# A four-layer graph network on one core: order of the first layer and its borders, and another form of the first layer's softmax weights

## The chip, the cores and the metric

One core of one Trainium2 chip. The metric is the device time of one execution in microseconds; the median over several executions is compared. The core has five engines with queues of their own: TensorE (PE, matmuls and transposes), VectorE (DVE), ScalarE (ACT), GpSimd (POOL, here the queue that issues indirect transfers) and SyncE (SP, here the queue that issues plain transfers).

## The reference

50,000 nodes with 128 features pass through four graph layers over 12,500 edges, sorted by target node. Each layer's result is added to its input and normalized over the features.

```python
x = _layernorm(x + L0(x, edges, edge_weight, edge_attr))   # attention with a softmax over the edges of a target
x = _layernorm(x + L1(x, src, dst))                        # mean of neighbours, two linear maps, relu
x = _layernorm(x + L2(x, src, dst, edge_type_8))           # one of 8 matrices for each edge, summed by target
x = _layernorm(x + L3(x, src, dst, edge_type_3, node_type_3))
...
# L0, for the 4 heads of an edge:
alpha = (q_s[dst] + k_s[src] + e_s) * inv_sqrt_c + gate * edge_weight
alpha = jnp.where(alpha >= 0, alpha, 0.2 * alpha)
ex = jnp.exp(alpha - amax[dst])
denom = segment_sum(ex, dst)
out = segment_sum(v[src] * ex / (denom[dst] + 1e-16), dst) + bias
```

## The kernel before

**Two streams of work.** The dense stream takes all nodes in 100 blocks of 500 rows (125 partitions x 4 x 128 features) through all four layers, for nodes without edges and as a base for the rest. Step d of it (numbered in the code as `d`) works on three blocks at once: block d enters layer one, block d - 3 (LAG) layer two and three, block d - 6 the last layer. The edge stream takes the 12,500 edges in 25 chunks of 500, layer by layer: 25 chunks of the first layer, then 25 of the second, and so on. The two streams are interleaved by hand: two dense steps go with each first-layer chunk, one with each chunk of the second and third layer, none with the fourth. Every engine has its own written-out program; semaphores tie them together. Nothing is planned by a scheduler: the order of calls in each engine's block is the order of work.

**First layer, one chunk c.** GpSimd gathers source and target rows (`sources0`, `targets0`, four indirect transfers each) and issues five more for the table of slots. TensorE transposes the rows (`turn_sources0`, `turn_targets0`, L1380) into one PSUM bank `pt`, ScalarE takes them out (`evacuate_sources` to `st`, `evacuate_targets` to `dt`, L1145), and TensorE adds three products into `pc`: `score_features`, `score_sources` (L1494) and `score_targets` (L1500). ScalarE writes 0.2 of the scores (`slopes0`, L1151), VectorE takes the larger (L842). The softmax is computed as a running one along the edges: L844 scans the running maximum (in the profile every scan has its helper's line, L831), which a mask of -1e30 resets where a new target begins; L845 subtracts the score from the maximum of the edges before. ScalarE splits the difference d in two by Relu (`differences0`, L1156 and L1157) and takes two exponents (`weights0`, L1162 and L1163): the old sum is scaled by one of them (`wb`) and the new term by the other (`wa`). Two more scans (`weight_sums`, `value_sums`) carry the sums on. TensorE turns them back (`back0`, L1514, L1518), ScalarE takes out the denominators (`sums0`), VectorE divides and adds (`target_rows0`, L867 to L871).

**The dense step.** VectorE's `read(d)` adds the bias (L791), takes the result of layer two out of PSUM bank group `po` (L796), selects the node type's result (L799, L800) and forms the last sum (L802); `measure` and L764, L767 make the variances. ScalarE's `first_roots` turns these into seeds of 1/sqrt, VectorE's `scales` (L778 to L781) finishes them, ScalarE normalizes rows (L1074). TensorE's `dense_turns` transposes (`turn_rt`, `turn_xt`), ScalarE evacuates (`evacuate_rt`, `evacuate_xt`), and `dense_products` writes `po`: `biased_slots` (L1386) and the type products (L1391) need `read(d + 2)` to be through and `rt`; `z_products` (L1451) need `xt`. `read(d + 3)` waits for them.

**What sets the order around the change.** In the first layer's loop each engine runs this for chunk c:

```python
# TensorE, the end of a chunk           # ScalarE, the ends of a chunk
turn_xt(2 * c + 1)                      first_roots(s, 8)
turn_targets0(c + 2)                    slopes0(c + 1)
score_targets(c + 2)                    ...
dense_products(2 * c + 1)               evacuate_xt(2 * c + 1)
                                        evacuate_targets(c + 2, 0, 0, dt, ACT.Copy)
```

VectorE's loop is: `source_rows0(c)` (L880), `read(2c)`, statistics, `target_rows0(c - 1)`, `read(2c + 1)`, statistics, `weight_sums(c)` (scan), `scales` (L778 on), `value_sums(c)` (scan), `scores(c + 1)` (L841 to L845).

**Borders.** After the last first-layer chunk ScalarE writes all rows and results before `only_dense(2 * EC)` takes `rt` out; the second layer's gathers wait for the last target rows in memory (`landed(1)`). Before the third layer TensorE runs `dense_products(d - 2)` ahead of `turns2(0)`. GpSimd gathers the node types of the targets (`types2`, array `ntd_all`, 100 transfers): 8 after the second layer's gathers, 3 in each of the third layer's 25 chunks, and the last 17 between the third layer's gathers and `landed(3)`, ahead of the fourth layer's. They are needed first at L1046, when the fourth layer begins. ScalarE runs the last `dense_chain` before it takes out `st` of the fourth layer's chunk 1.

## Time and profile before

| | |
|---|---|
| median of three executions | 1655.96 us (1653.0 to 1656.04) |
| the profiled execution | 1652.15 us, span 1650.4 us |
| mean granted TensorE clock | 0.929 of full |
| busy share of the span | PE 84%, DVE 86%, ACT 67%, POOL 75% |
| chain that ended last | PE 44%, DVE 32%, ACT 12%, issue 10% |

How to read it: a busy share is a mean over stages with different limits. PE is TensorE's matmul, PEld its weight load. In a timeline row the columns are the start in us, the duration in us, the engine, the line, the operation with output and inputs, how many were merged, and in brackets the idle time ahead of it with what ended it. `issue` as a releaser means that the profile shows nothing that was waited for. Instructions on one engine overlap a little, so the next may start before the last has ended. L12 is line 12 of the kernel before.

### The profile page before, as it was taken

What the parts mean: (1) busy time and instruction counts of PE and PEld (TensorE: products, weight loads), DVE (VectorE), ACT (ScalarE), POOL (GpSimd) and SP (SyncE); (2) the same over time, 40 slices, a digit from 0 to 9 for tenths busy, and PEclk for the clock granted to TensorE, in tenths of its full rate; (3) what the DMA queues carried; (4) which work ended last, traced back from release to release, by engine and by line L of the source; (5) the groups of instructions that cost most, each with busy time, mean ns of one, the idle gap of its engine ahead of it and who ended that gap; (6) DMA issues with size and microseconds to landing.
All of it is one profiled execution on the core that took longest, in us unless ns stands there. A gap on an engine that the chain in (4) does not pass through costs nothing.

```text
span 1650.4 us, 22899 instructions
## 1 busy us (share of the span) xinstructions
PE 1388.8 (84%) x6078; PEld 890.6 (54%) x6078; DVE 1419.0 (86%) x3056; ACT 1110.9 (67%) x2769; POOL 1230.3 (75%) x910
## 2 busy tenths in 40 slices
PE   3788877788778868777776899999996899999995
PEld 2455554555545546666665555555553455555552
DVE  5899899999899879999998799999995677777773
ACT  1678788887788787888888577777774344444441
POOL 7888888877777857888874567777778488888873
PEclk9798888988889879999998999999998899999997
DMA  7344444434444256767675455556554344344320
GB/s 172 94 100 102 111 109 110 112 91 115 111 113 105 58 139 177 189 179 192 182 187 149 131 149 164 156 157 165 151 133 111 83 97 96 96 97 97 96 70 20
DMA packets 165797, 205.06 MB, mean 124 GB/s; under 512 B 66825, under 2 KB 97920, under 8 KB 165668
## 3 DMA queue, kind: packets, MB, share of 16 engines
q1 hardware_dynamic: 108068, 179.45, 40.0%
q0 software_dynamic: 57600, 24.15, 9.0%
q8 instruction: 50, 0.82, 0.2%
q14 instruction: 79, 0.65, 0.2%
HBM read 147.12 MB, written 70.80 MB: 132 GB/s over the span
## 4 chain that ended last, share of the span: by engine, by line
PE 44%; DVE 32%; ACT 12%; issue 10%; POOL 1%; DMA 1%; SPq 0%; DVEq 0%; POOLq 0%; ACTq 0%
PE po L1391 23%; DVE bst L756 8%; DVE masked L969 6%; PE pt L1380 5%; PE pc L1500 3%; PE po L1386 3%; ACT x L1074 3%; DVE run L831 2%; PE po L1451 2%; DVE y L796 2%; DVE po L799 2%; DVE sel L802 2%; DVE po L800 2%; ACT do L1074 2%; PE pa L1672 1%
## 5 line engine op out<-in xcount | busy, mean ns | idle before, releaser
L536 POOL DMA_INDIRECT xs<-target_rows,slot_all x236 | 322.2, 1365 | 140.9 <-issue 60.9
L1074 ACT ACTIVATE x<-y,nmr,rst 125x128 f32<-125x128 f32 x800 | 322.5, 483 | 29.6 <-issue 18.4
L1391 PE MATMUL po<-wnt,rt 128*125 128x384 f32 x800 | 297.4, 518 | 0.0
L1380 PE MATMUL pt<-ident,x 125*128 125x125 f32 x800 | 122.3, 276 | 110.5 <-issue 110.5
L1391 PEld LDWEIGHTS po<-wnt,rt 128*125 128x125 f32 x800 | 162.7, 206 | 96.9 <-issue 21.2
L1391 PE MATMUL po<-wnt,run 128*125 128x384 f32 x600 | 201.5, 486 | 0.0
L543 POOL DMA_INDIRECT out_rows<-do,last_all x100 | 146.5, 1465 | 63.0 <-issue 40.6
L1380 PEld LDWEIGHTS pt<-ident,x 125*128 125x128 f32 x800 | 93.1, 145 | 148.4 <-issue 147.1
L536 POOL DMA_INDIRECT xs<-in_x,src_all x100 | 143.2, 1432 | 34.7 <-issue 33.8
L1074 ACT ACTIVATE do<-yd,nmr,rst 125x128 f32<-125x128 f32 x400 | 163.5, 483 | 5.4 <-DVE nmr L781 4.6
L1074 ACT ACTIVATE res<-sel,nmr,rst 125x128 f32<-125x128 f32 x400 | 163.7, 484 | 2.6 <-DVE nmr L781 1.8
L1627 PE MATMUL pb<-masked,wr 128*128 128x500 f32 x350 | 156.5, 588 | 2.2 <-DVE masked L969 2.2
L536 POOL DMA_INDIRECT slot_all<-slot_d,src_all x100 | 131.9, 1319 | 30.5 <-issue 30.5
L536 POOL DMA_INDIRECT ntd_all<-in_ntype,dst_all x100 | 129.4, 1294 | 30.5 <-issue 30.5
L543 POOL DMA_INDIRECT slot_d<-eid,last_all x100 | 128.5, 1285 | 30.5 <-issue 30.2
L756 DVE BATCH_NORM_STATS2 bst<-y 125x6 f32<-125x256 f32 x400 | 143.1, 420 | 3.8
L1391 PEld LDWEIGHTS po<-wnt,run 128*125 128x125 f32 x600 | 108.9, 188 | 68.7 <-issue 0.6
L1140 ACT ACTIVATE st<-pt 128x500 f32<-128x500 f32 x50 | 29.3, 585 | 142.1 <-issue 95.1
L536 POOL DMA_INDIRECT xdb<-target_rows,slot_all x64 | 86.6, 1352 | 44.2 <-issue 29.3
L536 POOL DMA_INDIRECT xd<-in_x,dst_all x68 | 94.9, 1396 | 27.2 <-issue 19.2
L1386 PE MATMUL po<-ball,ones_bf 128*125 128x384 bf16 x412 | 102.2, 379 | 13.0 <-DVE sel L802 13.0
L1451 PEld LDWEIGHTS po<-wab,xt 128*125 128x125 f32 x800 | 101.5, 188 | 19.8
(190 smaller groups left out, 3035.1 us busy)
## 6 DMA issues: line engine op xcount, KB each, us to landing
xin<-in_x SPq DMA_DIRECT2D x100, 224.0 KB
out_rows<-res SPq DMA_DIRECT2D x100, 224.0 KB
source_rows<-so SPq DMA_DIRECT2D x75, 224.0 KB
target_rows<-do SPq DMA_DIRECT2D x75, 224.0 KB
xs<-source_rows SPq DMA_DIRECT2D x59, 224.0 KB
same<-same_d SPq DMA_DIRECT2D x50, 250.0 KB
rel<-in_etype SPq DMA_DIRECT2D x50, 250.0 KB
xd<-target_rows SPq DMA_DIRECT2D x46, 224.0 KB
```

Of the source, the lines that this page charges most:

```text
L536: return nc.gpsimd.indirect_dma_start(out=to, out_offset=None, in_=table, in_offset=bass.IndirectOffsetOnAxis(ap=index, axis=0), bounds_ch ...
L543: return nc.gpsimd.indirect_dma_start(out=table, out_offset=bass.IndirectOffsetOnAxis(ap=index, axis=0), in_=of, in_offset=None, bounds_ch ...
L756: last = V.bn_stats(to, y[:, j:j + 2, :].rearrange("p j d -> p d j"))
L796: last = V.scalar_tensor_tensor(out=y1[(d - LAG) % 4][:, :, :], in0=of_z, scalar=0.0, in1=x1[(d - LAG) % 4][:, :, :], op0=ALU.max, op1=ALU ...
L969: V.scalar_tensor_tensor(out=masked[:, r, :], in0=rel[b][:, :], scalar=float(r), in1=st[:, :], op0=ALU.is_equal, op1=ALU.mult).then_inc(q[ ...
L1074: last = A(to[:, j, :], y[:, j, :], ACT.Identity, scale=rst[s][:, k:k + 1], bias=nmr[s][:, k:k + 1])
L1380: last = nc.tensor.transpose(tile_of(to, j), rows_[:, j, :], ident[0:R, 0:R])
L1386: mm(po[0:R, j * 512:j * 512 + NT * D], ones_bf[:, 0:R], ball[:, :, :].rearrange("k s d -> k (s d)"), start=True, stop=False, skip_group_c ...
L1391: last = mm(po[0:R, j * 512:j * 512 + NT * D], left(j), wnt[:, k, :, :].rearrange("k t d -> k (t d)"), start=start, stop=stop, skip_group_ ...
L1451: last = mm(po[0:R, j * 512 + NT * D:(j + 1) * 512], xt[:, j, :], wab[:, 0, :], start=False, stop=True, skip_group_check=True)
L1500: mm(pc[:, 0:C], qs[:, :], dt[:, :], start=False, stop=True).then_inc(q["pA"], 1)
L1627: mm(pb[:, 0:C], wr[:, r, :], masked[:, r, :] if r else st[:, :], start=r == 0, stop=r == REL - 1).then_inc(q["pM"], 1)
```

## The change

- VectorE's form of the weights (`scores`): the mask is used at the edge itself, not one edge ahead. The scan is now max(run + mask, score). Then three operations: `wb` = run before + mask, completed before the next; `wa` = score - run; `wb` = `wb` - run. ScalarE takes the exponent of each; the two Relus and their semaphore `eR` are gone, and with them one of the two transfers of the mask array, and a memset.
- ScalarE's loop in the first layer: `evacuate_targets(c + 1)` comes after `first_roots` of chunk c, in place of the end of the chunk before.
- TensorE's loop in the first layer: the second dense product of a chunk is split; biased slots and type products come before `turn_targets0(c + 2)`, the z products between it and `score_targets(c + 2)`.
- End of the first layer on ScalarE: `evacuate_rt`, `evacuate_xt` and `first_roots` of the next dense step come between the rows and before the results.
- Second to third layer on TensorE: `turns2(0)` before `dense_products(d - 2)`.
- GpSimd: 15 of the type gathers are issued in the second layer's chunks 20 to 24, so that 2 are left of the 17 ahead of `landed(3)`.
- Third to fourth layer on ScalarE: `evacuate_sources(1, 3, 0)` before the last `dense_chain`.

```diff
@@ -66,7 +66,7 @@
...
     d_rows = [nc.dram_tensor(f"target_rows{i}", [E, D], F32).ap() for i in (1, 2, 3)]
     same_d = nc.dram_tensor("same_d", [1, E], F32).ap()
-    start_d = nc.dram_tensor("start_d", [1, E + 1], F32).ap()
+    start_d = nc.dram_tensor("start_d", [1, E], F32).ap()
     rdeg_d = nc.dram_tensor("rdeg_d", [1, E], F32).ap()
@@ -172,7 +172,7 @@
...
         SOONER = 10
 
-        SINGLE = ("tS tD eS eD eL pA pB pR vA vE vL eX eR nS nD nF yb eN sc", "tS tD eS eD pR vA nS nD rd vF",
+        SINGLE = ("tS tD eS eD eL pA pB pR vA vE vL eX nS nD nF yb eN sc", "tS tD eS eD pR vA nS nD rd vF",
                   "tS eS pM pR vA vM nD nF nS", "tS tD eS eD pM pR vM vA eX vN nD rd bs xb")
@@ -240,8 +240,7 @@
...
             sp.wait_ge(s_prep, 1)
             row = lambda a: a.rearrange("o (p t) -> (o p) t", t=PM)
-            sp.dma_start(row(start_d[0:1, 0:E]), start_p[:, :]).then_inc(s_scr, 16)
-            sp.dma_start(start_d[0:1, E:E + 1], start_p[0:1, 0:1]).then_inc(s_scr, 16)
+            sp.dma_start(row(start_d), start_p[:, :]).then_inc(s_scr, 16)
             sp.dma_start(w1t[:, :, :], W1T).then_inc(s_w2, 16)
@@ -255,7 +254,7 @@
...
                 sp.dma_start(ea[b][0:ED, :], eattrT[:, cols(c)]).then_inc(q["aux"][b], 16)
                 sp.dma_start(ea[b][ED:ED + 1, :], eweight[0:1, cols(c)]).then_inc(q["aux"][b], 16)
-                sp.dma_start(aux[b][:, :], start_d[0:1, bass.ds(c * C + 1, C)].broadcast_to([D, C])).then_inc(q["aux"][b], 16)
+                sp.dma_start(aux[b][:, :], to_all(start_d, c)).then_inc(q["aux"][b], 16)
 
@@ -269,7 +268,7 @@
...
                     sp.dma_start(rows(d_rows[0])[c][part, :], flat(do[b])[part, :]).then_inc(q["stD"][b], 16)
 
-            sp.wait_ge(s_scr, 32)
+            sp.wait_ge(s_scr, 16)
             features0(0)
@@ -633,6 +632,9 @@
...
                         pool.wait_ge(s_slot[k], 16 * T * (n - 1))
                     slots1(i, i + 1, s_slot[k])
+                if SOONER * T + 3 * c >= EC * T:
+                    types2(typed, typed + 3)
+                    typed += 3
             types2(typed, typed + 2 * T)
@@ -694,7 +696,6 @@
...
             V.memset(carry[:, :], 0.0)
             step(V.memset(run[:, :, :], 0.0))
-            V.memset(run[:, 0, 0:1], -BIG)
             V.tensor_scalar(start_p[:, :], same_p[:, :], -1.0, BIG, ALU.add, ALU.mult).then_inc(s_prep, 1)
@@ -841,8 +842,10 @@
...
                 V.tensor_tensor(score, score, pc[:, 0:C], ALU.max).then_inc(q["vL"], 1)
                 dve.wait_ge(q["vL"], c + 1)
-                step(scan(run, 0, score, aux[b][:, :], ALU.max, ALU.add))
-                V.tensor_tensor(wb, run[:, 0, 0:C], score, ALU.subtract).then_inc(q["vE"], 1)
+                step(scan(run, 0, aux[b][:, :], score, ALU.add, ALU.max))
+                step(V.tensor_tensor(wb, run[:, 0, 0:C], aux[b][:, :], ALU.add))
+                V.tensor_tensor(wa, score, run[:, 0, 1:C + 1], ALU.subtract)
+                V.tensor_tensor(wb, wb, run[:, 0, 1:C + 1], ALU.subtract).then_inc(q["vE"], 1)
 
@@ -1123,8 +1126,12 @@
...
             def dense_chain(d):
 
+                first_roots(chain_of(d) % 2, 4)
+                chain_rows(d)
+
+            def chain_rows(d):
+
                 k = chain_of(d)
-                first_roots(k % 2, 4)
                 act.wait_ge(s_ln, k + 1)
@@ -1150,17 +1157,11 @@
...
                 A(score, pc[:, 0:C], ACT.Copy, scale=0.2).then_inc(q["eL"], 1)
 
-            def differences0(c):
+            def weights0(c):
                 q = ph[0]
                 act.wait_ge(q["vE"], c + 1)
-                A(wa, wb, ACT.Relu)
-                A(wb, wb, ACT.Relu, scale=-1.0).then_inc(q["eR"], 1)
-
-            def weights0(c):
-                q = ph[0]
-                act.wait_ge(q["eR"], c + 1)
-                A(wb, wb, ACT.Exp, scale=-1.0)
-                A(wa, wa, ACT.Exp, scale=-1.0).then_inc(q["eX"], 1)
+                A(wb, wb, ACT.Exp)
+                A(wa, wa, ACT.Exp).then_inc(q["eX"], 1)
 
@@ -1183,13 +1184,14 @@
...
             evacuate_targets(0, 0, 0, dt, ACT.Copy)
             slopes0(0)
-            differences0(0)
             weights0(0)
...
                 s = chain_of(2 * c) % 2
                 first_roots(s, 8)
+                if c >= 1 and there(c + 1):
+                    evacuate_targets(c + 1, 0, 0, dt, ACT.Copy)
                 if there(c + 1):
@@ -1199,7 +1201,6 @@
...
                 if there(c + 1):
                     evacuate_rt(2 * c)
-                    differences0(c + 1)
                     evacuate_xt(2 * c)
@@ -1217,12 +1218,13 @@
...
                     act.wait_ge(s_tail, 1)
                     target_rows0(c, TAIL, 0)
+                    evacuate_rt(2 * EC - 2)
                     source_rows0(c, s)
+                    evacuate_xt(2 * EC - 2)
+                    first_roots(chain_of(2 * EC) % 2, 4)
                     results_of(2 * c, s, 2)
                     results_of(2 * c + 1, s, 3)
-                if there(c + 2):
-                    evacuate_targets(c + 2, 0, 0, dt, ACT.Copy)
-            only_dense(2 * EC)
+            chain_rows(2 * EC)
             evacuate_dense(2 * EC - 1)
@@ -1350,8 +1352,8 @@
...
             messages3(0)
             targets3(0)
+            evacuate_sources(1, 3, 0)
             dense_chain(NC + 2 * LAG - 1)
-            evacuate_sources(1, 3, 0)
             act.wait_ge(s_x1, NC)
@@ -1553,10 +1555,16 @@
...
                         score_sources(c + 2)
                     turn_xt(2 * c + 1)
+                    if 2 * c + 1 >= LAG:
+                        type_products(2 * c + 1)
+                    else:
+                        pe.wait_ge(s_read, 2 * c + 4)
+                        biased_slots()
                     if there(c + 2):
                         turn_targets0(c + 2)
+                    z_products(2 * c + 1).then_inc(s_z, 1)
+                    if there(c + 2):
                         score_targets(c + 2)
-                    dense_products(2 * c + 1)
 
@@ -1628,9 +1636,9 @@
...
             d = block_of(1, EC)
             dense_turns(d - 2)
-            dense_products(d - 2)
             pe.wait_ge(ph[1]["rd"], EC)
             turns2(0)
+            dense_products(d - 2)
             relations2(0, range(REL // 2))
...
```

## Rows read from the trace of the kernel before

**Rows 1.** Busy time in stretches: us, then PE, PEld, DVE, ACT, POOL; clock, DMA, GB/s.
```profile
80.00:560.00 480.00, 393.27 (x1760) 253.70 (x1758) 437.55 (x898) 385.78 (x976) 385.39 (x281) 0.87 0.44 105
...
615.00:885.00 270.00, 212.96 (x1423) 173.36 (x1423) 261.16 (x657) 234.15 (x598) 211.22 (x159) 1.00 0.68 180
...
935.00:1245.00 310.00, 302.86 (x1225) 181.33 (x1224) 301.12 (x656) 225.35 (x578) 223.13 (x167) 1.00 0.58 152
...
1295.00:1640.00 345.00, 334.81 (x1110) 190.15 (x1108) 262.49 (x464) 134.69 (x289) 256.98 (x183) 0.99 0.35 85
```

**Rows 2.** Waits, 60 to 560 us: total us, times, longest.
```profile
DVE tmp L778 <- issue: 14.1, 13, 4.0
...
DVE y L796 <- PE po L1451: 11.2, 19, 1.2
...
DVE tmp L778 <- ACT seed L1083: 7.2, 7, 1.1
```

**Rows 3.** Timeline of VectorE, first layer.
```profile
311.15 1.26 DVE L831 TENSOR_TENSOR_SCAN run<-masked,run,aux 128x500 f32<-128x500 f32 x1
...
313.04 0.68 DVE L880 TENSOR_TENSOR so<-xs,bias_bc 125x512 f32<-125x512 f32 x1
...
324.74 0.69 DVE L802 SCALAR_TENSOR_TENSOR sel<-x,po 125x512 f32<-125x512 f32 x1
...
330.02 0.19 DVE L778 SCALAR_TENSOR_TENSOR tmp<-seed 125x32 f32<-125x32 f32 x1 [1.01 <-ACT seed L1083]
...
332.80 0.67 DVE L842 TENSOR_TENSOR masked<-masked,pc 128x500 f32<-128x500 f32 x1
...
563.50 0.67 DVE L842 TENSOR_TENSOR masked<-masked,pc 128x500 f32<-128x500 f32 x1
```

**Rows 4.** Timeline of ScalarE, first layer.
```profile
329.02 0.59 ACT L1145 ACTIVATE dt<-pt 128x500 f32<-128x500 f32 x1 [1.25 <-PE pt L1380]
```

**Rows 5.** Timeline of TensorE, first layer.
```profile
318.26 0.81 PE L1386 MATMUL po<-ball,ones_bf 128*125 128x384 bf16 x4
...
321.50 1.04 PE L1451 MATMUL po<-wab,xt 128*125 128x128 f32 x8
322.80 1.01 PE L1494 MATMUL pc<-st,ks 128*128 128x500 f32 x2
...
329.66 2.03 PE L1500 MATMUL pc<-dt,qs 128*128 128x500 f32 x2 [0.68 <-ACT dt L1145]
331.49 1.48 PE L1386 MATMUL po<-ball,ones_bf 128*125 128x384 bf16 x4
...
335.96 1.04 PE L1451 MATMUL po<-wab,xt 128*125 128x128 f32 x8
```

**Rows 6.** Stretch view of TensorE alone: us, PE busy, granted clock, DMA, GB/s.
```profile
328.00:330.00 2.00, 1.32 (x5) 0.50 0.87 267
```

**Rows 7.** Timeline of GpSimd, first layer.
```profile
311.87 1.62 POOL L536 DMA_INDIRECT xs<-in_x,src_all  x1 [0.30 <-issue]
```

**Rows 8.** Timeline of TensorE, first border.
```profile
599.40 1.06 PE L1380 MATMUL pt<-ident,x 125*128 125x125 f32 x4 [11.45 <-issue]
```

**Rows 9.** Group of the type gathers; then timelines of GpSimd and TensorE, second border.
```profile
L536 POOL DMA_INDIRECT ntd_all<-in_ntype,dst_all x100 | 129.4, 1294 | 30.5 <-issue 30.5
...
900.88 1.27 POOL L536 DMA_INDIRECT xs<-target_rows,slot_all  x1 [17.16 <-DMA target_rows<-do]
...
910.83 1.46 PE L1386 MATMUL po<-ball,ones_bf 128*125 128x384 bf16 x4
...
916.62 0.59 PE L1380 MATMUL pc<-ident,xs 125*128 125x125 f32 x4
```

**Rows 10.** Timelines of GpSimd and TensorE, third border.
```profile
1262.04 1.27 POOL L536 DMA_INDIRECT xdb<-target_rows,slot_all  x1 [0.30 <-issue]
...
1269.68 1.07 PE L1380 MATMUL pt<-ident,xdb 125*128 125x125 f32 x4 [4.09 <-issue]
...
1285.89 2.03 PE L1672 MATMUL pa<-st,wet 128*128 128x500 f32 x2 [7.40 <-ACT st L1140]
```

## The prediction

> **What bounds the kernel now.** I read the stages first: the view by stretches [rows 1] splits the span into four layers with short borders between them. In the first layer (80 to 560 us) VectorE is busy 437.6 of 480 us, TensorE 393.3, ScalarE 385.8 and GpSimd 385.4, with TensorE granted 0.87 of full clock; in the second and third VectorE has 261.2 of 270 and 301.1 of 310 us; in the fourth TensorE has 334.8 of 345. So VectorE is nearest to the limit in three layers and TensorE in the last. Time saved on another engine counts only where one of these waits for it.
>
> Next I read the first layer's waits [rows 2]: in 500 us VectorE waits 14.1 + 7.2 us for the seeds of L778 and 11.2 us for the z products at L796. Its timeline [rows 3] gives the period: L842 starts at 332.80 and at 563.50, ten chunks apart, 23.07 us each. The waits are 32.5 us over 21.7 such periods, 1.50 a chunk, so VectorE's own work is about 21.57 us. Short delays hidden by overlapping instructions are not in that sum; between 21.4 and 21.6 is my bracket, 21.45 my value.
>
> Then ScalarE and TensorE [rows 4 to 6]: ScalarE stands 1.25 us before the evacuation dt at 329.02, in front of the seeds, so the seeds come late. TensorE runs the type products only after score_targets, and part of this at the lower of its two clocks: the same two 500-column matmuls take 1.01 us at 322.80 and 2.03 us at 329.66 (1.2 GHz, granted clock 0.50, where before it was 2.4). At the borders I read TensorE's and GpSimd's timelines [rows 8 to 10].
>
> **First layer, VectorE's arithmetic.** The scan (1.26 us at 311.15) keeps its length. Before, one subtraction follows it and then L880, which does not wait for that subtraction: from the scan's end, 312.41, to L880 at 313.04 are 0.63 us, 0.60 for the subtraction and 0.03 for the hand-over. Now an addition that must complete comes first, then two subtractions. The addition costs a whole operation of this size, 0.68 us, and a hand-over, 0.72 with rounding; each subtraction 0.60 [rows 3]. Added: 0.72 + 0.60 = 1.32 us a chunk. ScalarE loses two Relus of the size of dt (0.59 us in [rows 4]); that is worth nothing by itself, since ScalarE already waits. VectorE's floor is then 21.45 + 1.32 = 22.77 us.
>
> **First layer, the order.** Moving the dt evacuation behind first_roots puts the seeds in front of ScalarE's wait, and they hide under the weight scan. Moving the type products ahead of turn_targets0 removes the z wait, which also lets back0 start earlier. So the 1.50 us of waits go. What is late next is the chain that now hangs from the second read: the read's last instruction (324.74, ends 325.43) releases type_products(2c+1); then come the target transposes, dt on ScalarE, score_targets, the slopes, and L842. From there to L842 are 332.80 - 325.43 = 7.37 us, of which 1.01 is the wait for the seeds at 330.02 [rows 3]; room 6.4 us. The chain at the high clock [rows 4, 5]: 3.24 us (biased slots and types, 318.26 to 321.50) + 0.55 (four transposes, half the 1.07 of the slow ones in [rows 10]) + 0.59 (dt) + 1.01 (scores) + 0.59 (slopes, same shape as dt) + about 0.2 for hand-overs = 6.2 us, with z beside dt. It just fits. At the lower clock in part it does not: the same products took 4.47 us (331.49 to 335.96), 1.23 more, and the scores 1.02 more. So the stall is 0 to 2.2 us a chunk. The clock fell before after TensorE had stood for most of the time from 323.8 (the end of the row at 322.80) to 329.66 [rows 5, 6]; in the new order it pauses before the same products, for the rt evacuation and the read, but more briefly. I take 0.45 us, nearer to the clean row, because the score matmuls should mostly run at the high clock again. Period 22.77 + 0.45 = 23.22 against 23.07: +0.15 x 22 chunks = +3 us. Bounds: -7 us (no stall) and +42 us (2.2 in every chunk).
>
> The three chunks of the ramp I cost at nothing, within 2 us either way. The single start-mask transfer instead of two, the memset gone and the shifted mask are before the first chunk, beside the weight loads; nothing, and at most 1 us either way.
>
> **A lock on GpSimd.** GpSimd issues 13 indirect transfers a chunk, 385.4 us / 281 = 1.37 us each [rows 1] and 0.31 between two [rows 9]: 21.8 us of the 23.07. The one that starts at 311.87, inside the scan, took 1.62 us [rows 7] against 1.29 on the mean for the type gathers [rows 9], so a scan holds it up by about 0.33 us. The Trainium skill, "SBUF — State Buffer", section "Who interferes with whom", says that a VectorE instruction with two SBUF inputs blocks a GpSimd instruction that reads SBUF, and for its full length. The trace agrees in that row. By the row, one more delay of 0.33 us fits in GpSimd's slack and the sum stays. By the rule, all 1.3 us of new two-input work could be added to GpSimd, 21.8 + 1.3 = 23.1 us a chunk, and the first layer could not win anything: +1 us in place of -7 us for the case without stalls.
>
> **First border.** TensorE stood 11.45 us before the transpose at 599.40 [rows 8], because the rt evacuation came after all rows and results. It now comes some 4 us earlier, and the dense products with it. But the second layer's first transposes need GpSimd's gathers, which wait for the last target rows, and those are not moved. ScalarE's own work also stays in the way. Only the 1 us by which results no longer delay its next rows is left: -0.9 us; bounds 0 and -4.
>
> **Second border.** turns2(0) moves ahead of the dense products that ran from 910.83 to 916.62: 5.8 us earlier at most [rows 9]. Against it: 15 type gathers move into the end of the second layer, where GpSimd had only 8; each costs 1.29 + 0.31 = 1.60 us. Twelve of the 15 and the 8 follow the last row gather. The 8 before ended 17.16 us ahead of 900.88, when the first gather started, at 883.72; twelve more and a last row gather that starts some 0.7 us later make 883.72 + 12 x 1.60 + 0.7 = 903.6, so the first gather comes 2.8 us later. A group of four gathers needs 7.64 us from its start to TensorE (1262.04 to 1269.68, [rows 10]), so turns2(0) can run at 911.3, 5.3 us sooner. Then the displaced dense products push the relation products and with them st of the next chunk, which takes back some 1.6 us: -3.7 us; bounds 0 and -5.8. The layer behind is full on VectorE, so this gain stays.
>
> **Third border [rows 10].** Of the 17 type gathers between the layers 15 are gone, 24 us of GpSimd. The first row gather (1262.04) can go as soon as the last rows have landed. TensorE stood 4.09 us before its transpose at 1269.68 and was busy before, so 4.1 us is the most that this brings; I take all of it. Second, st of chunk 1 is taken out before the last dense chain: TensorE's 7.40 us before 1285.89 shrink to an evacuation and hand-over, 0.8 us: -6.6 us. Behind these pauses the matmuls ran at 1.2 GHz (2.03 us for two); some of them now run at 2.4 GHz: -0.8 us. Together -11.5 us; bounds -4 (only one of the two) and -16. The fourth layer is bound by TensorE [rows 1], so its start shifts the end one for one.
>
> **Sum.** +3 - 0.9 - 3.7 - 11.5 = -13.1 us. The profiled execution took 1652.15 us (span 1650.4), so 1639.1 by it. It is 3.8 us below the median of 1655.96, and two of the three runs shown lie at 1656; the forecast goes by the median: 1655.96 - 13.1 = 1642.9, rounded to 1642 because the sum has more room below.
>
> **Rivals.**
> (1) No stall: the first layer reaches VectorE's floor, -7 us, total -23: 1633. For it: the chain fits by 0.2 us at the high clock. Against it: that margin, and GpSimd's lock. Chance 0.20.
> (2) The lock makes GpSimd the bound, first layer +1 us, total -15: 1641; told from the forecast only by whether the transfers are long. Chance 0.06.
> (3) The borders' gains are hidden anyway: the second and third layers' queues (row stores, loads, ScalarE's order) hold them to -4 us in the third border and nothing else; with +3 us: 1655, or 1651 if half of the second border stays. For it: each border moves one thing out of several. Against it: TensorE's waits of 7.40 and 4.09 us name just what is moved. Chance 0.13.
> (4) The other side, slower: in the first layer the chain from the read over type products, dt, scores and slopes runs at the lower clock in every chunk. At 1.6 us of stall: (22.77 + 1.6 - 23.07) x 22 = +28.6, total +12.5: 1668. It decides from 1.05 us a chunk, where 22 x (22.77 + 1.05 - 23.07) = 16.5 eats the borders' 16.1. For it: the products follow TensorE's pauses. Against it: these are shorter than before. Chance 0.11.
> The forecast has 0.50.
>
> **How the numbers follow.** 0.2%, about 3.3 us, is what can be told from no change. Faster: 0.50 + 0.20 + 0.06 and 0.07 of case 3, 0.83; same: 0.06 of case 3; slower: 0.11. The likeliest case's own range is 1634 to 1650 (stall 0.1 to 0.8 us, third border -8 to -15). The range of 8 in 10 takes in most of cases 1 and 3: 1629 to 1655.
>
> **What would show it.** VectorE: L778 without a wait in the first layer, 1.32 us more between the scan and L880's start. L842 waiting on ScalarE's slopes: my stall; over 1.05 us a chunk, case 4. Period near 22.8: case 1. GpSimd without any wait for VectorE and a period equal to VectorE's: case 2. Borders: TensorE's pauses before the last first-layer transpose, before the first relation product's source and before the fourth layer's second message product shorter by some 4, 5 and 6.6 us; GpSimd's first third-layer gather 2.8 us later relative to the layer's end. The forecast is wrong if the first layer moves by more than 15 us or the third border brings less than 8.

## The result, and the profile after

The changed kernel takes 1660.03 us (median of 7 runs, 1658.3 to 1662.74) against 1654.32 us of the kernel before in as many runs beside it (1653.0 to 1656.04). The ratio is 1.0041 with a 95% interval of 1.0031 to 1.0050: slower by 5.7 us, where 13.1 us less and 1642 were forecast. The profiled execution took 1658.97 us, span 1657.2.

The starts of the scans (VectorE, one per chunk and layer, listed by line for each kernel) mark the stages in both traces. Each stretch runs from the start of one scan to that of another:

| stretch | before, us | after, us | difference | forecast |
|---|---|---|---|---|
| first layer, first to last scan | 533.2 | 554.7 | +21.5 | +3 |
| first border | 48.6 | 47.5 | -1.1 | -0.9 |
| second layer | 274.5 | 276.5 | +2.0 | 0 |
| second border | 46.0 | 46.2 | +0.2 | -3.7 |
| third layer | 312.9 | 313.1 | +0.2 | 0 |
| third border and fourth layer | 365.3 | 350.1 | -15.2 | -11.5 |

The start (-0.8) and the tail (0) make it +6.8 us of span. The first and the third border did what was forecast or more, the second gained nothing, and the first layer took it all back.

The view by stretches of the changed kernel (columns as in [rows 1]; the later three lie where the layers lie now):

```profile
80.00:560.00 480.00, 372.73 (x1696) 241.36 (x1693) 443.13 (x900) 351.02 (x894) 372.43 (x269) 0.86 0.44 103
636.00:905.00 269.00, 212.55 (x1431) 173.76 (x1431) 259.32 (x652) 231.34 (x590) 212.21 (x161) 1.00 0.70 180
957.00:1265.00 308.00, 300.71 (x1216) 180.26 (x1214) 299.30 (x650) 225.17 (x577) 217.97 (x162) 1.00 0.57 151
1302.00:1647.00 345.00, 334.19 (x1108) 189.81 (x1106) 266.40 (x468) 135.24 (x291) 260.13 (x185) 0.99 0.36 88
```

In the first row no engine is full: VectorE stands for 37 of 480 us, although it has 1.3 us more to do in each chunk. In the waits of the changed kernel (60 to 560 us, columns as in [rows 2]) VectorE's seeds are gone, and among the long entries are waits of ScalarE for TensorE and of TensorE for ScalarE:

```profile
ACT xt L1120 <- PE pt L1382: 54.6, 23, 3.0
...
ACT dt L1152 <- PE pt L1382: 39.3, 21, 3.7
PE pa L1508 <- ACT den L1171: 36.4, 21, 1.9
...
ACT masked L1158 <- PE pc L1502: 25.1, 21, 1.2
```

One period of it, ScalarE first (the timelines of the changed kernel; L1158 slopes, L1077 rows and results, L1171 denominators, L1163 and L1164 the exponents):

```profile
320.68 0.59 ACT L1158 ACTIVATE masked<-pc 128x500 f32<-128x500 f32 x1 [1.20 <-PE pc L1502]
...
324.24 1.64 ACT L1077 ACTIVATE res<-sel,nmr,rst 125x128 f32<-125x128 f32 x4
...
325.84 0.16 ACT L1171 ACTIVATE den<-pa 125x4 f32<-125x4 f32 x1
...
329.01 0.59 ACT L1120 ACTIVATE xt<-pt 128x500 f32<-128x500 f32 x1 [2.55 <-PE pt L1382]
...
331.17 0.59 ACT L1147 ACTIVATE st<-pt 128x500 f32<-128x500 f32 x1 [0.55 <-PE pt L1382]
...
337.81 0.56 ACT L1114 ACTIVATE rt<-pt 128x500 f32<-128x500 f32 x1
...
342.79 0.59 ACT L1152 ACTIVATE dt<-pt 128x500 f32<-128x500 f32 x1 [1.81 <-PE pt L1382]
344.57 0.59 ACT L1158 ACTIVATE masked<-pc 128x500 f32<-128x500 f32 x1 [1.20 <-PE pc L1502]
```

and TensorE (L1382 turns, L1508 values, L1491 the features' scores, L1388 and L1393 biases and types, L1453 z, L1502 the targets' scores):

```profile
323.48 0.79 PE L1382 MATMUL pt<-ident,x 125*128 125x125 f32 x4
326.14 2.01 PE L1508 MATMUL pa<-st,wv 128*128 128x500 f32 x2 [1.87 <-ACT den L1171]
327.94 1.04 PE L1382 MATMUL pt<-ident,x 125*128 125x125 f32 x4
328.77 1.88 PE L1491 MATMUL pc<-ea,es 65*128 65x500 f32 x2
...
338.47 0.62 PE L1382 MATMUL pt<-ident,x 125*128 125x125 f32 x4 [1.97 <-issue]
338.93 0.82 PE L1388 MATMUL po<-ball,ones_bf 128*125 128x384 bf16 x4
339.58 2.74 PE L1393 MATMUL po<-wnt,rt 128*125 128x384 f32 x8
342.16 0.59 PE L1382 MATMUL pt<-ident,xdb 125*128 125x125 f32 x4
342.59 1.04 PE L1453 MATMUL po<-wab,xt 128*125 128x128 f32 x8
343.46 1.07 PE L1502 MATMUL pc<-dt,qs 128*128 128x500 f32 x2
```

Read as one chain these rows close on themselves: slopes, rows, results and denominators on ScalarE (320.68 to 326.0); values and the turn of x1 on TensorE (326.14 to 328.98); xt, the exponents, st (after 0.55 us of wait for TensorE), rows, the edge rows and rt on ScalarE (329.01 to 338.37); turn, types and the targets' turn on TensorE (338.47 to 342.75); dt; the scores; and the next slopes at 344.57, 23.89 us on. No link of it is on VectorE, whose own work is 22.73 us (the period less its waits of 0.87 at L842 and 0.29 at L797). It waits at the end of the chain:

```profile
345.19 0.15 DVE L842 COPY run<-run 128x1 f32<-128x1 f32 x1 [0.87 <-ACT masked L1158]
```

TensorE's granted clock in it (columns as in [rows 6]). TensorE had stood 1.54 us ahead of the turning back at 322.18; the clock falls shortly before 324, at the end of the short work that follows and before the pause for the denominators begins. The values, a turn and the features' scores run at the lower clock, the types' products no longer do.

```profile
322.18 0.67 PE L1516 MATMUL pb<-ident,run 128*125 128x128 f32 x4 [1.54 <-DVE masked L843]
```

```profile
322.00:324.00 2.00, 1.82 (x16) 0.95 0.15 33
324.00:326.00 2.00, 0.27 (x2) 0.50 0.15 32
...
328.00:330.00 2.00, 2.00 (x7) 0.50 0.52 75
330.00:332.00 2.00, 2.00 (x11) 0.84 0.96 216
```

At the third border of the changed kernel the two pauses of [rows 10] are gone or small, and the products run at 2.4 GHz:

```profile
1286.88 0.62 PE L1382 MATMUL pt<-ident,xdb 125*128 125x125 f32 x4
...
1293.97 1.10 PE L1680 MATMUL pa<-st,wet 128*128 128x500 f32 x2 [0.68 <-ACT st L1147]
```

At the second, GpSimd works through the moved types until the first gather, and TensorE gets its rows 11.64 us after that gather's start, at the lower clock (the rows that answer to [rows 9]):

```profile
924.06 1.27 POOL L535 DMA_INDIRECT ntd_all<-in_ntype,dst_all  x1 [0.30 <-issue]
925.64 1.27 POOL L535 DMA_INDIRECT xs<-target_rows,slot_all  x1 [0.30 <-issue]
```
```profile
937.28 1.07 PE L1382 MATMUL pc<-ident,xs 125*128 125x125 f32 x4 [3.78 <-issue]
```

### The profile page after: what moved, and what is told of

Its sections match the earlier page's. It is cut to its first block, busy times and chain, and to the rows that moved or that the text cites. A ratio compares the mean times of both kernels' runs of the same rounds, so it can differ in the third digit from the quotient of the medians.

```text
span 1657.2 us, 22897 instructions
## 1 busy us (share of the span) xinstructions
PE 1381.7 (83%) x6078; PEld 890.1 (54%) x6078; DVE 1450.1 (88%) x3105; ACT 1087.2 (66%) x2719; POOL 1235.3 (75%) x910
## 4 chain that ended last, share of the span: by engine, by line
PE 45%; DVE 35%; ACT 9%; issue 9%; DMA 1%; POOL 0%; SPq 0%; DVEq 0%; POOLq 0%; ACTq 0%
PE po L1393 23%; DVE bst L757 9%; DVE masked L972 6%; PE pt L1382 5%; ACT x L1077 4%; DVE run L832 3%; PE pa L1508 3%; PE po L1453 3%; ACT res L1077 2%; DVE po L801 2%; DVE sel L803 2%; PE pc L1491 2%; PE po L1388 2%; DVE y L797 2%; DVE po L800 2%
## 5 line engine op out<-in xcount | busy, mean ns | idle before, releaser
L1077 ACT ACTIVATE x<-y,nmr,rst 125x128 f32<-125x128 f32 x800 | 322.4, 482 | 28.9 <-DVE nmr L782 28.9
L1393 PE MATMUL po<-wnt,rt 128*125 128x384 f32 x800 | 283.2, 499 | 0.0
L1382 PE MATMUL pt<-ident,x 125*128 125x125 f32 x800 | 137.1, 300 | 101.7 <-issue 101.7
L1393 PE MATMUL po<-wnt,run 128*125 128x384 f32 x600 | 201.5, 487 | 0.0
L1393 PEld LDWEIGHTS po<-wnt,rt 128*125 128x125 f32 x800 | 153.6, 195 | 88.2 <-issue 7.8
L1382 PEld LDWEIGHTS pt<-ident,x 125*128 125x128 f32 x800 | 102.9, 156 | 152.4 <-issue 151.6
L535 POOL DMA_INDIRECT xs<-in_x,src_all x100 | 148.8, 1488 | 34.9 <-issue 33.9
L1077 ACT ACTIVATE do<-yd,nmr,rst 125x128 f32<-125x128 f32 x400 | 163.4, 482 | 5.4 <-DVE nmr L782 5.4
L1077 ACT ACTIVATE res<-sel,nmr,rst 125x128 f32<-125x128 f32 x400 | 163.7, 483 | 2.6 <-DVE nmr L782 2.6
L1393 PEld LDWEIGHTS po<-wnt,run 128*125 128x125 f32 x600 | 109.1, 188 | 68.6 <-issue 0.6
L535 POOL DMA_INDIRECT xd<-in_x,dst_all x68 | 93.3, 1372 | 37.5 <-DVE yd L874 19.3
L832 DVE TENSOR_TENSOR_SCAN run<-aux,run,masked 128x500 f32<-128x500 f32 x100 | 120.4, 1246 | 0.9
L1120 ACT ACTIVATE xt<-pt 128x500 f32<-128x500 f32 x100 | 58.3, 583 | 76.0 <-PE pt L1382 76.0
```

Source lines behind the costliest of these rows:

```text
L535: return nc.gpsimd.indirect_dma_start(out=to, out_offset=None, in_=table, in_offset=bass.IndirectOffsetOnAxis(ap=index, axis=0), bounds_ch ...
L832: return V.tensor_tensor_scan(m[:, k, 1:C + 1], data0, data1, m[:, k, 0:1] if start is None else start, op0, op1)
L1077: last = A(to[:, j, :], y[:, j, :], ACT.Identity, scale=rst[s][:, k:k + 1], bias=nmr[s][:, k:k + 1])
L1120: A(xt[:, :, :], by_tile(pt), ACT.Copy, bias=1.0).then_inc(s_xt, 1)
L1382: last = nc.tensor.transpose(tile_of(to, j), rows_[:, j, :], ident[0:R, 0:R])
L1393: last = mm(po[0:R, j * 512:j * 512 + NT * D], left(j), wnt[:, k, :, :].rearrange("k t d -> k (t d)"), start=start, stop=stop, skip_group_ ...
```

## The experiments

Two theories at the start. A: the new order in the first layer lengthens the loop through ScalarE and TensorE. B: the three VectorE operations do. Medians below are of each kernel's runs (4 to 11); the kernel before stood between 1652.7 and 1653.2 us beside them.

**The parts one by one.** Three kernels each take some hunks of the change on top of the kernel before, with all that belongs to them; of each a few lines.

Borders alone, the hunks at the three borders:

```diff
             targets3(0)
+            evacuate_sources(1, 3, 0)
             dense_chain(NC + 2 * LAG - 1)
-            evacuate_sources(1, 3, 0)
```

> The kernel before with all the changes at the borders (ScalarE's order at the end of the first layer, the type gathers of the second layer, the turns of the third layer's first chunk, the early evacuation in the fourth) and the first layer's loop and weights left as they were. Theory A (the first layer's loop lost what the borders gave): the first layer keeps its 533 us from the first to the last scan, the fourth layer with its border gives the 15 us that the changed kernel shows, the first border 1, the second nothing: 1638 to 1641 us, a ratio of 0.991. Rival B (the fourth layer's gain was an echo of the first layer's later end, since loads and gathers had more time): the border's gain is under 8 us here, and the kernel stays above 1646.

Measured 1638.3, ratio 0.9907 (0.9892 to 0.9922). From the last scan of the third layer to the last of the fourth are 350.4 us, as in the changed kernel: the gain there is the borders' own.

Weights alone, the hunks in `scores`, `weights0` and the start marks:

```diff
-                V.tensor_tensor(wb, run[:, 0, 0:C], score, ALU.subtract).then_inc(q["vE"], 1)
+                step(V.tensor_tensor(wb, run[:, 0, 0:C], aux[b][:, :], ALU.add))
+                V.tensor_tensor(wa, score, run[:, 0, 1:C + 1], ALU.subtract)
+                V.tensor_tensor(wb, wb, run[:, 0, 1:C + 1], ALU.subtract).then_inc(q["vE"], 1)
```

> The kernel before with the new form of the first layer's weights alone (three VectorE operations for one, two exponents for two cuts and two exponents, the marks not shifted by one), old order everywhere. Theory A (the new order of dt, types and targets turned TensorE's clock down in another place and lengthened the loop; the arithmetic costs what VectorE had free): 0 to +8 us, a period of 23.1 to 23.4 us, and ScalarE's two cuts gone shorten its chain. Rival B (the arithmetic alone costs the 21 us: 1.32 us of VectorE for each of 24 chunks, less what its waits gave, behind the scan and ahead of the exponents): +18 to +25 us, a period of 23.8 to 24.1.

Measured 1653.47, ratio 0.9999 (0.9990 to 1.0008): nothing, and B is refuted. The stretch from 80 to 560 us shows VectorE at 459.7 busy us (437.6 in [rows 1]):

```profile
80.00:560.00 480.00, 395.24 (x1758) 254.86 (x1756) 459.68 (x937) 365.77 (x932) 374.44 (x278) 0.87 0.46 104
```

Periods are 22.5 to 23.6 us (22.35 to 23.5 before). In one chunk of four VectorE now waits for nothing, and that period, 22.52 us, is its own work; in the others its waits are 0.33 to 0.68 us, where they were 1.0 to 1.8.

Order alone, the loop's hunks on ScalarE (dt behind the roots) and TensorE (types, targets' turn, z, scores), both shown by halves further below:

> The kernel before with the first layer's new order alone (ScalarE takes dt out after the roots of the next chunk, TensorE puts the targets' turn between the types' products and z, and the targets' scores after z), old weights, old borders. Theory A (the order is what lengthens the loop): +10 to +20 us, TensorE at the low clock from the values' products on and not in the types' products, and ScalarE waiting over 2 us for the turn of x1 ahead of xt. Rival B (the arithmetic alone costs it): within 3 us of the kernel before. Rival C (only both together lengthen it, as VectorE's slack is gone and the chain of dt, scores and slopes is long): within 5 us here and within 8 us with the weights alone.

Measured 1673.05, ratio 1.0119 (1.0103 to 1.0134): +19.8 us. The three parts are -14.9, +0.3 and +19.8, in sum +5.2; together they measured +5.7. Most periods here are 23.88 to 23.90 us, those of the changed kernel, though VectorE has 1.3 us less to do: it just waits more (1.60 us at L796 and 0.86 at L841). ScalarE's two cuts, which this kernel still has, fit into its wait for xt, 1.53 us instead of 2.55. So neither VectorE's nor ScalarE's own work sets the period.

The changed kernel with the denominators taken out sooner:

```diff
                 rows_of(2 * c, s, (4, 0))
+                sums0(c)
                 if there(c + 1):
                     results_of(2 * c, s, 2)
-                sums0(c)
```

> The changed kernel with one move: ScalarE takes the denominators out before it writes the results of the dense block, not after (1.64 us earlier). Theory A (the pause that TensorE makes for the denominators ahead of the values' products is what lets its clock fall, and the products and turns at the low clock make ScalarE wait for xt 2.55 us in every chunk): the pause of 1.87 us is down to 0.3 or less, the wait for xt under 1.5 us, the period 23.89 down to between 22.8 and 23.2, the whole 15 to 24 us under the changed kernel: 1636 to 1645. Rival B (the loop is bound by VectorE's arithmetic and by the chain dt, scores, slopes): the period stays at 23.7 or above, 1655 to 1660.

Measured 1651.35, ratio 0.9994 (0.9983 to 1.0004), some 8 us under the changed kernel by the ratios, where I expected 15 to 24. The wait for xt is down to 1.20 and 0.75 us in the two chunks of the middle, and the periods are no longer one value but 22.7 to 24.4 us. So the link is on the chain. But my reason was wrong: the pause for the denominators is 0.5 us or none (1.87 before this edit), and still the values run at the lower clock for most of their length in 14 of 17 chunks (1.6 to 2.01 us for two; 1.08 in the other three). That pause is not what lets the clock fall.

**The clock, and the halves of the order.** In the changed kernel TensorE now repeats a turn to fill its pause; the argument says how often, and the signal goes with the last:

```diff
-                    turn_rt(2 * c)
+                    turn_rt(2 * c, 5)
                     values0(c + 1)
```

> The changed kernel with its first turn of x3 in each chunk issued five times in a row instead of once (the same values into the same tile, signalled after the last), so that TensorE works through most of the 1.87 us in which it otherwise waits for the denominators. Nothing comes earlier by it on any engine. Theory A (what the pause costs is TensorE's clock: the values' products, a turn and the features' scores at 1.2 GHz take 2.4 us more than at 2.4 GHz and hand ScalarE xt 2.55 us late): the granted clock stays at 1.00 between the turn and the sources' turn, the period goes from 23.89 to between 22.8 and 23.3, the whole to 1636 to 1648. Rival B (the clock is an effect and not a cause, what counts is when the denominators come out): the period stays at 23.8 or above and the whole at 1657 to 1662.

Measured 1664.26, ratio 1.0067 (1.0052 to 1.0081), slower still, and outside both expectations. Two neighbouring chunks of its trace differ. In one the types' products run at 1.2 GHz and VectorE waits 1.77 us; in the next at 2.4 GHz and it waits 0.33:

```profile
196.31 1.49 PE L1388 MATMUL po<-ball,ones_bf 128*125 128x384 bf16 x4
197.58 3.80 PE L1393 MATMUL po<-wnt,rt 128*125 128x384 f32 x8
...
206.44 4.00 PE L1382 MATMUL pt<-ident,x 125*128 125x125 f32 x20
...
221.06 0.81 PE L1388 MATMUL po<-ball,ones_bf 128*125 128x384 bf16 x4
221.71 2.74 PE L1393 MATMUL po<-wnt,rt 128*125 128x384 f32 x8
```
```profile
204.25 0.15 DVE L842 COPY run<-run 128x1 f32<-128x1 f32 x1 [1.77 <-ACT masked L1158]
...
227.32 0.15 DVE L842 COPY run<-run 128x1 f32<-128x1 f32 x1 [0.33 <-ACT masked L1158]
```

The chunks take 24.69 and 23.07 us in turn for most of the layer. The difference is in the products ahead of the targets' turn, which take 1.7 us longer at the lower clock; where it falls is worth 1.6 us a chunk.

The edit also did harm of its own. The clock fell just after the start of the repeated turns (at 206.5), behind a pause of 1.54 us that ended at 205.13. At the lower clock the twenty turns take 3.5 to 4.4 us, in 19 of the 20 chunks from 86 to 547 us (2.33 in the other one), and so last longer than the pause that they were to fill: the denominators are out at 208.95, the values start at 210.27, and ScalarE waits 1.52 us for the last turn before it can take rt out. So this run shows what the clock is worth in the types' products. It doesn't show what the chain would be if the clock had stayed up, and neither theory is settled by its time.

ScalarE's half of the order, on the kernel before:

```diff
                 first_roots(s, 8)
+                if c >= 1 and there(c + 1):
+                    evacuate_targets(c + 1, 0, 0, dt, ACT.Copy)
...
-                if there(c + 2):
-                    evacuate_targets(c + 2, 0, 0, dt, ACT.Copy)
```

> The kernel before with ScalarE's half of the new order alone: dt is taken out after the roots of the next chunk and not before them; TensorE's order, weights and borders as before. Theory A (TensorE's half of the order lengthens the loop): no loss here; VectorE's wait for the roots (0.7 to 1.1 us in the chunks of before) is gone, dt is 0.5 us later: -12 to +2 us. Rival B (ScalarE's half lengthens it: scores and slopes come later by the roots' 0.5 us and everything behind them on ScalarE): +12 to +20 us, a period near 23.9.

Measured 1652.28, ratio 0.9998 (0.9989 to 1.0007): no loss. VectorE's wait for the seeds has become one for the slopes (0.77 us at L841), the periods are those of the kernel before.

TensorE's half, on the kernel before:

```diff
                     turn_xt(2 * c + 1)
+                    if 2 * c + 1 >= LAG:
+                        type_products(2 * c + 1)
...
                     if there(c + 2):
                         turn_targets0(c + 2)
+                    z_products(2 * c + 1).then_inc(s_z, 1)
+                    if there(c + 2):
                         score_targets(c + 2)
-                    dense_products(2 * c + 1)
```

> The kernel before with TensorE's half of the new order alone: the targets' turn stands between the types' products and z, the targets' scores after z; ScalarE's order as before, so that the roots now stand behind a dt that comes later. Theory A (this half lengthens the loop, since dt, scores and slopes follow 3 us of types' products): +15 to +25 us, and VectorE waits over 1.5 us for the roots in every chunk. Rival B (the half on ScalarE is what costs): within 4 us of the kernel before.

Measured 1680.19, ratio 1.0161 (1.0148 to 1.0175): +27.5 us, a little over the range. This half is the loss. The periods are 23.89 again, with VectorE waiting 2.17 us for the seeds behind a late dt. ScalarE's half takes some 8 us of it back in the order as a whole.

The changed kernel with the whole order undone (these two hunks taken back):

> The changed kernel with only the first layer's order undone (new weights, all borders as changed). Theory A (the order is the whole loss, and the parts add up): 0.9999 times 0.9907 of before, 1638 us give or take 2, 21 under the changed kernel. Rival B (weights and borders share a slack that each alone still finds): 1643 or more.

Measured 1638.21, ratio 0.9909 (0.9894 to 0.9925). The parts add up, and the order costs 21.8 us in the changed kernel.

**Which products.** TensorE's half puts types ahead of the targets' turn, and z ahead of the targets' scores. One kernel takes the first back:

```diff
                     turn_xt(2 * c + 1)
+                    if there(c + 2):
+                        turn_targets0(c + 2)
                     if 2 * c + 1 >= LAG:
                         type_products(2 * c + 1)
...
-                    if there(c + 2):
-                        turn_targets0(c + 2)
                     z_products(2 * c + 1).then_inc(s_z, 1)
```

> The changed kernel with the targets' turn back ahead of the types' products of the odd dense block; z still stands ahead of the targets' scores, ScalarE's order and all else as changed. Theory A (dt, and the scores and slopes behind it, are late because the turn follows 3.4 us of types' products): dt is 3 us earlier, but the scores still follow types and z; of the 21 us at most half comes back, 1648 to 1660, if what counts is when the scores come, and all of it, 1637 to 1643, if what counts is when the turn comes (it holds the tile from which ScalarE takes dt out ahead of everything of the next chunk). I take the first.

Measured 1725.7, ratio 1.0448 (1.0431 to 1.0466), 67 us slower than the changed kernel by the ratios, where I had expected a gain. It undoes half of a move and is worse than the whole: the targets' turn now waits for xt (1.44 us), which the types had covered, the types come behind it at the lower clock (3.74 us for eight, 2.74 in the changed kernel), and the scores still follow all of it. ScalarE, and VectorE behind it, wait for the scores:

```profile
ACT masked L1158 <- PE pc L1502: 101.4, 19, 6.0
DVE run L842 <- ACT masked L1158: 64.8, 18, 5.0
```

The other takes the second back:

```diff
+                    if there(c + 2):
+                        score_targets(c + 2)
                     z_products(2 * c + 1).then_inc(s_z, 1)
-                    if there(c + 2):
-                        score_targets(c + 2)
```

> The changed kernel with the targets' scores ahead of z in the odd dense block, so that only the types' products still stand ahead of the targets' turn. Theory A (it is these 3.4 us, at the head of the chain of targets' turn, dt, scores and slopes, that lengthen the loop; z runs while ScalarE takes dt out): ScalarE's wait for the slopes' scores is 1.2 to 1.9 us as before, the whole within 6 us of the changed kernel's 1660. Rival B (z ahead of the scores is the costly half): the first layer gets back 15 us or more, 1645 or less.

Measured 1659.37, ratio 1.0033 (1.0021 to 1.0045), within 2 us of the changed kernel; the slopes' wait is 1.20 us as expected. In sum z ahead of the scores costs nothing, though the loop is another one: periods of 25.3, 23.4 and 23.0 us in turn, and the values at the higher clock in about half of the chunks. By both kernels what counts is that the types stand between the turn of x1 and the scores. A kernel with z alone there was not tried.

**Shortening the chain instead.** If the chain from rt to the slopes binds, the remedy is on ScalarE: on the kernel with changed borders, old weights and TensorE's old order,

```diff
                     source_rows0(c, s)
+                    evacuate_rt(2 * c + 1)
                     if c >= 1:
                         target_rows0(c - 1, s, 7)
-                    evacuate_rt(2 * c + 1)
-                    results_of(2 * c + 1, s, 3)
                     evacuate_xt(2 * c + 1)
+                    results_of(2 * c + 1, s, 3)
```

> The kernel before with the changed borders and another change of order in the first layer, on ScalarE alone: in the odd dense block rt is taken out ahead of the edge targets' rows and xt ahead of the results (old weights, TensorE's order as before). The turn of x1 should come 1.6 us earlier and the targets' turn 1.6 us or more. Theory A (the loop follows the chain xt, targets' turn, dt, scores, slopes, and the clock falls in TensorE's pause ahead of it): VectorE's waits of 1.5 us go down to 0.7 or less, the period from 23.07 to between 21.8 and 22.6, the whole to 1612 to 1630. Rival B (the period follows the dense blocks' chain of z, read, roots and rows, which this doesn't shorten): 1636 to 1640, as the borders alone.

Measured 1607.78, ratio 0.9724 (0.9711 to 0.9738), better than the range. The turn of x1 waits 0.53 us (2.06 in the kernel before), and in two of three chunks VectorE waits for nothing: a period of 21.2 to 21.4 us, its own work, and 22.3 in the third. Which of the two moves, rt or xt, carries it was not tried.

```profile
331.08 0.57 ACT L1114 ACTIVATE rt<-pt 128x500 f32<-128x500 f32 x1
331.55 1.65 ACT L1077 ACTIVATE do<-yd,nmr,rst 125x128 f32<-125x128 f32 x4
333.09 0.58 ACT L1120 ACTIVATE xt<-pt 128x500 f32<-128x500 f32 x1
```
```profile
331.76 0.62 PE L1390 MATMUL pt<-ident,x 125*128 125x125 f32 x4 [0.53 <-issue]
```

The same with the weights' hunks on top:

> The kernel with changed borders and rt and xt taken out earlier (1607.8 us, a period of 21.3 in which VectorE waits for nothing), now with the new form of the weights too. Theory A (the arithmetic cost nothing in the old loop only because that was bound by the hand-overs between ScalarE and TensorE; here VectorE is the bound): VectorE's 1.28 us more for each of 24 chunks are paid in full, a period of 22.6 to 22.8, 1635 to 1641. Rival B (the three operations overlap with each other and with waits, and ScalarE's two cuts less give it back): within 6 us of 1607.8.

Measured 1628.82, ratio 0.9846 (0.9832 to 0.9859): 20 to 21 us more than without them, between the two expectations. Periods are 22.51 to 22.61 us, 1.28 more where VectorE alone binds, and 22.93 in six of them, where it waits for z 0.34 us and not 0.7 to 0.85 any more. So the arithmetic has its price of 1.3 us in every chunk in which VectorE waits for nothing; over the 24 periods it is 0.94 on the mean (525.3 us for the layer against 502.7).

**The second border.** The 15 early types go back, and the third layer takes four a chunk:

```diff
-                if SOONER * T + 3 * c >= EC * T:
-                    types2(typed, typed + 3)
-                    typed += 3
...
-                types2(typed, typed + 3)
-                typed += 3
+                types2(typed, typed + 4)
+                typed += 4
```

> The kernel with new weights and changed borders and the first layer's old order, with one change at the second border: the 15 early type gathers go back out of the second layer's end, and the third layer's chunks take four each instead of three, so that none is left ahead of the fourth layer. Theory A (the early types push the third layer's first gather back by 3.1 us and so eat the gain of the moved turns): the second border is 3 to 4 us shorter, the fourth layer's unchanged, 1634 to 1636. Rival B (the second border is bound elsewhere, by ScalarE's and VectorE's dense chain, and the gather's time doesn't count): within 1.5 us of that kernel's 1638.

Measured 1632.93, ratio 0.9883 (0.9868 to 0.9898), a little under the range, against 0.9909 for the same kernel with early types. The second border is 42.0 us (45.7 with them, 46.0 before), the fourth layer with its border 350.3. So the turns' move is worth 4.0 us at the second border and the early types cost 3.7 of them in this pair. Over all kernels that moved the turns the border takes 43.6 to 46.2 us in nine with the early types and 42.0 and 42.2 in the two without, so the early types cost 1.4 to 4.2.

The last two kernels' gains together (this edit and the one on rt and xt, old weights):

> The fastest of what was tried, together: old weights, changed borders but the type gathers spread over the third layer's chunks by fours, rt and xt taken out earlier in the first layer. Theory A (the second border's 4 us and the first layer's 30 add up, being far apart in time): 1602 to 1605. Rival B (the earlier end of the first layer already used what the second border has): 1606 to 1609.

Measured 1602.96 us, ratio 0.9693 (0.9679 to 0.9707): the fastest, 50.3 us under the kernel before and 57 under the changed one.

## Why the prediction was wrong

**First layer, the order: this step failed.** The forecast gave the layer +3 us, and it took +21.5; that is 18.5 of the 18.8 us by which the whole missed. The stall was 0.45 us in the forecast and is 1.16 (0.87 at L842, 0.29 at L797), the period 23.89 us and not 23.22. The last 20 periods make 16.7 of the 21.5 us; the first four make 4.8, 4.1 of it in the third, where I had put the ramp at nothing. The size of the stall was within its bounds; what was wrong is how I got it. I started the chain at the second read. Its links have the predicted length: from the types' first product (338.93) to the end of the slopes (345.16) are 6.23 us, 6.2 in the forecast, and at the high clock as assumed. But it doesn't start at the read, which is done at 338.02. It starts at the turn of x1, which waits for rt on ScalarE until 338.37, and I had left both out: the products begin 0.91 us after the read's end, a term that the forecast had at nothing. And rt is late because the chain closes on itself: its own end delays the rows, those the denominators, those the values and so on to rt. I costed an open chain hung from an engine that I took for the bound, where a loop without that engine was longer. The loop was to be seen in the profile before: ScalarE's waits there (0.24 to 1.75 us, four in a period) already named TensorE in every case.

The same points of a period, in the kernel before:

```profile
331.73 0.59 ACT L1151 ACTIVATE masked<-pc 128x500 f32<-128x500 f32 x1 [1.75 <-PE pc L1500]
...
338.32 0.17 ACT L1170 ACTIVATE den<-pa 125x4 f32<-125x4 f32 x1
...
340.23 0.58 ACT L1117 ACTIVATE xt<-pt 128x500 f32<-128x500 f32 x1
...
341.72 0.58 ACT L1140 ACTIVATE st<-pt 128x500 f32<-128x500 f32 x1
...
348.34 0.57 ACT L1111 ACTIVATE rt<-pt 128x500 f32<-128x500 f32 x1
...
352.17 0.59 ACT L1145 ACTIVATE dt<-pt 128x500 f32<-128x500 f32 x1 [1.25 <-PE pt L1380]
...
354.88 0.59 ACT L1151 ACTIVATE masked<-pc 128x500 f32<-128x500 f32 x1 [1.75 <-PE pc L1500]
```

| from start to start on ScalarE | before, us | after, us | difference |
|---|---|---|---|
| slopes to denominators | 6.59 | 5.16 | -1.43 |
| denominators to xt | 1.91 | 3.17 | +1.26 |
| xt to st | 1.49 | 2.16 | +0.67 |
| st to rt | 6.62 | 6.64 | +0.02 |
| rt to dt | 3.83 | 4.98 | +1.15 |
| dt to slopes | 2.71 | 1.78 | -0.93 |
| period | 23.15 | 23.89 | +0.74 |

The new order did remove what it was to remove: the denominators no longer wait 1.31 us for the turning back, and the seeds and the slow scores (2.03 us, now 1.07) are gone from between dt and the slopes. Against these 2.36 us stand 1.15 for the types ahead of dt and 1.93 between the denominators and st, where TensorE now works at the lower clock.

The clock was the second error in that step. That it falls around a pause was read rightly; I looked only at whether the types' products would still be hit. They are not: the values, the turn of x1 and the features' scores are (2.01, 1.04 and 1.88 us, where they were 1.08, 0.59 and 1.01). TensorE's links in the loop are 3.0 us from the denominators to xt, 0.55 ahead of st, 4.4 from rt to dt and 1.2 from dt to the slopes, and the work of the first two is for the most part at the lower clock.

**VectorE's arithmetic: right in what it adds.** 1.32 us was forecast for the two added operations, 1.28 to 1.30 measured. As the floor 22.77 us was forecast; the changed kernel's period less its waits is 22.73, but chunks in which VectorE waits for nothing take 22.52 (21.24 without the added operations), so the floor was some 0.25 us too high. The arithmetic is worth nothing in the old order, where VectorE waited 1.0 to 1.8 us in each chunk; where it waits for nothing it costs its full price.

**Rivals.** The fourth case came closest, but its mechanism is not what happened: the chain from the types to the slopes runs at the higher clock. L842 waits 0.87 us, under the case's deciding point of 1.05; only with the 0.29 at L797 is it passed. The third case, that the borders' gains would be hidden, is ruled out by the borders alone (-14.9 us). GpSimd was the bound nowhere, since it still waits for VectorE in the changed kernel (19.3 us in nine waits for yd). Between the two kernels with the shortened chain, without and with the added operations, GpSimd's mean transfer goes from 373.8 / 284 = 1.32 us to 381.1 / 285 = 1.34, some 0.3 us for the 13 of a chunk, and chunks of 22.5 us occur. The Trainium skill, "SBUF — State Buffer", section "Who interferes with whom", has a VectorE instruction with two SBUF inputs block a GpSimd instruction that reads SBUF, for its full length; it adds that `tensor_tensor` was not seen to stall transfers, for a reason that it calls inferred. By the estimate with the full length the period could not have gone under 23.1 us, and the runs go under it.

**First border: right as far as it can be told**, -1.1 us in the changed kernel for -0.9, with TensorE's pause down from 11.45 to 6.83 us. Over all kernels this border takes 48.3 to 49.3 us in the five without its edits and 46.6 to 49.0 in the eleven with them. The second layer's +2.0 us was not forecast. Kernels with the changed borders have 275.2 to 276.7 us there, the five without them 274.5 to 274.8. The early types are not the main cause: the two kernels without them have 275.4 and 275.2. Which edit does it stays open.

**Second border: the mechanism right, one term wrong.** The first gather came 3.1 us later in relation to the last scan (2.8 forecast). But I gave a group of gathers 7.64 us to TensorE, from the third border; here it was 11.64, so the turn came 1.0 us sooner in relation to the last scan and not 5.3. Without the early types it came 5.1 us sooner and was worth 4.0.

**Third border: right in kind, too small.** -15.2 for -11.5. The two pauses went as computed (4.09 to none, 7.40 to 0.68); the 3.7 us more lie within my bound of -16, and the term that was too small is the clock, for which I had taken 0.8 us. From the last scan of the third layer to the type products that follow the second group of message products (1290.40 before, 1296.59 after) are 44.2 us before and 28.4 after, 15.8 less. Pauses make 10.5 of that; the other 5.3 are the same matmuls taking less time, such as the first two of the first group:

```profile
1271.48 2.04 PE L1672 MATMUL pa<-st,wet 128*128 128x500 f32 x2 [0.74 <-ACT st L1140]
```
```profile
1288.24 1.11 PE L1680 MATMUL pa<-st,wet 128*128 128x500 f32 x2 [0.73 <-ACT st L1147]
```

## What to carry to other kernels

When two engines hand work back and forth, add up the loop through both, waits left out, before asking which engine is busiest; a move that shortens an engine's work or removes its wait gains nothing if it lengthens that loop, and moving short evacuations ahead of long independent rows can gain much (30 us here, for two of them together). In such a loop put the long products behind the short link that the other engine waits for. And price each part of a change alone: here two parts worth -15 and 0 hid behind one of +20.

## What was not expected of the hardware

In each period that I looked at TensorE's clock fell at least once (granted 0.50), and periods settle on fixed values: mostly 23.87 to 23.90 us in three kernels of different work (the order alone, TensorE's half alone, the changed kernel), 24.69 and 23.07 in turn with the repeated turns, 25.3, 23.4 and 23.0 in turn with the scores first. My reading, which no run shows by itself, is that a change in one link can cost nothing or several times its size, by where the lower clock falls next.

Twenty transposes without a gap did not keep the clock up, as it fell 0.1, 0.5 and 0.9 us after their start in three chunks, behind the pause ahead of them. But in two of these it came back inside the row (at 210.0 and at 353.3, the rows being 206.44 to 210.44 and 349.44 to 353.43), with nothing but transposes on TensorE since it had fallen.
